# A recommender tower on one core: the first table part ahead of the ids, the first ids and the first one-hot in halves

## What is computed

```python
e = jnp.stack([tbl_0[ids[:, 0]], ..., tbl_39[ids[:, 39]]], axis=1)
xi = e[:, iidx, :]
xj = e[:, jidx, :]
z = jnp.einsum('bpd,pde,bpe->bp', xi, bilinear_matrices, xj)
h = jnp.concatenate([z, dense_ctx], axis=1)
h = jnp.maximum(h @ W_top1 + b_top1, 0.0)
h = jnp.maximum(h @ W_top2 + b_top2, 0.0)
y = h @ W_top3
```

## Time and profile before

| | |
|---|---|
| median of 3 runs | 189.72 us (189.65 to 190.01) |
| the profiled execution's own time | 189.45 us |
| its span, first to last instruction | 187.6 us |
| mean granted TensorE clock | 0.991 |
| busy PE, DVE, POOL, ACT | 93%, 79%, 56%, 28% of the span |

### The profile page before, as it was taken

One profiled execution on the slowest core, in us unless ns is written; L12 is line 12 of the kernel. 1 busy time (PEld: TensorE's weight loads), 2 busy tenths in 40 slices (PEclk: granted clock), 3 DMA queues, 4 the chain that ended last, 5 costly groups with the idle time before them and its releaser, 6 DMA issues.

```text
span 187.6 us, 4092 instructions
## 1 busy us (share of the span) xinstructions
PE 174.1 (93%) x1766; PEld 59.9 (32%) x1766; DVE 148.9 (79%) x147; ACT 52.9 (28%) x52; POOL 105.8 (56%) x114
## 2 busy tenths in 40 slices
PE   6789788889999999999999999799999997998992
PEld 6434323233332233232323323223323242332340
DVE  1898999989599899899899999768899985770502
ACT  3875596898100201112110111102110111111501
POOL 2687777877877777777777777778600022202000
PEclk9969999999999999999999999999999999999999
DMA  5996130341055970220000010000000000000000
GB/s 153 350 410 254 17 98 14 108 124 19 14 153 102 330 285 14 73 106 18 13 15 14 14 17 11 14 18 12 3 0 0 3 0 0 5 0 0 3 0 0
DMA packets 7786, 13.07 MB, mean 70 GB/s; under 512 B 2164, under 2 KB 4728, under 8 KB 7768
## 3 DMA queue, kind: packets, MB, share of 16 engines
q1 hardware_dynamic: 4552, 11.15, 17.2%
q0 software_dynamic: 3072, 1.58, 4.8%
q10 hardware_dynamic: 144, 0.08, 0.3%
HBM read 12.67 MB, written 0.00 MB: 68 GB/s over the span
## 4 chain that ended last, share of the span: by engine, by line
PE 84%; ACT 8%; DVE 3%; DMA 2%; issue 2%; DVEq 0%; ACTq 0%
PE ps_t L679 27%; PE ps_z L693 27%; PE ps_x L727 9%; PE ps_x L642 7%; PE ps_t L738 4%; PE ps_t L673 3%; ACT hot_act L508 3%; ACT hot_act L510 3%; DMA ids<-ids_oh 2%; PE ps_t L713 2%; PE ps_x L654 2%; PE ps_z L642 1%; PE ps_t L706 1%; DVE hot_dve L556 1%; PE ps_t L642 1%
## 5 line engine op out<-in xcount | busy, mean ns | idle before, releaser
L596 DVE TENSOR_TENSOR prod<-ps_t,xt 128x1024 f32<-128x1024 f32 x100 | 116.7, 1218 | 18.3 <-PE ps_t L679 15.6
L485 POOL DMA_INDIRECT emb<-tbl,idx x96 | 94.5, 985 | 32.8 <-issue 29.0
L679 PE MATMUL ps_t<-xt,w_sb 32*128 32x512 f32 x360 | 54.3, 640 | 0.0
L693 PE MATMUL ps_z<-prod,ones 128*32 128x512 f32 x400 | 53.3, 605 | 0.0
L493 POOL TENSOR_TENSOR late_z<-late_z,tbl_oh 128x512 f32<-128x512 f32 x8 | 10.2, 1289 | 30.6 <-ACT tbl_oh L537 30.6
L727 PE MATMUL ps_x<-late_z,late_w 128*32 128x256 f32 x320 | 22.6, 379 | 2.0 <-ACT tbl_oh L537 2.0
L679 PEld LDWEIGHTS ps_t<-xt,w_sb 32*128 32x128 f32 x360 | 16.6, 183 | 22.5 <-issue 15.0
L556 DVE TENSOR_SCALAR hot_dve<-ids,ramp 128x2048 bf16<-128x2048 int16 x26 | 18.6, 763 | 3.7 <-DMA ids<-ids_oh 3.7
L693 PEld LDWEIGHTS ps_z<-prod,ones 128*32 128x32 f32 x400 | 7.9, 108 | 38.2 <-DVE prod L596 22.1
L727 PEld LDWEIGHTS ps_x<-late_z,late_w 128*32 128x32 f32 x320 | 10.3, 110 | 20.9 <-issue 19.0
L508 ACT ACTIVATE hot_act<-ids,neg_ramp 128x2048 bf16<-128x2048 int16 x8 | 15.9, 1992 | 2.7 <-DMA ids<-ids_oh 2.7
(11 more groups left out here) (64 smaller groups left out, 92.1 us busy)
## 6 DMA issues: line engine op xcount, KB each, us to landing
ids<-ids_oh SPq DMA_DIRECT2D x4, 512.0 KB, 7.0
emb<-tbl,idx POOLq DMA_INDIRECT x96, 2.3
late_w<-w SPq DMA_DIRECT2D x1, 1280.0 KB, 8.4
tbl_oh<-small_tables SPq DMA_DIRECT2D x2, 512.0 KB, 8.0
w_sb<-w_pairs SPq DMA_DIRECT2D x1, 704.0 KB
tbl_oh<-small_tables SPq DMA_DIRECT2D x1, 640.0 KB, 11.3
w_sb<-w_pairs SPq DMA_DIRECT2D x1, 640.0 KB
w_sb<-w_pairs SPq DMA_DIRECT2D x1, 576.0 KB, 4.5
```

The costliest lines, as they stand in the source:

```text
L485: nc.gpsimd.indirect_dma_start(emb[:, n % E_RING, t, u * D:(u + 1) * D], None, tables[field], bass.IndirectOffsetOnAxis(ap=idx[:, at:at + ...
L596: nc.vector.tensor_tensor(prod[:, g % PROD_RING, :].rearrange("p (i b) -> p i b", i=2), ps_t[PAIR[g]][:, :].rearrange("p (i b) -> p i b", ...
L679: last = nc.tensor.matmul(o, w_sb[s * D:(s + 1) * D, at:at + P], xt[s * D:(s + 1) * D, kk, :], start=True, stop=True)
L693: last = nc.tensor.matmul(ps_z[q * D:(q + 1) * D, :], ones[:, v * D:(v + 1) * D], prod[:, t // 2 % PROD_RING, t % 2 * B:(t % 2 + 1) * B], ...
```

## The change

Block 0's ids come as two transfers, of two fields each (256 KB): the first on ACT's queue ahead of `idx`, the second on SP's. SP issues table part 0 first and the second half of the ids behind it; the rest of its order stays. DVE does the split of part 0 ahead of its first one-hot, and that one-hot as two instructions of 128 x 1024, each after its own half. TensorE waits for both (the first half has a semaphore of its own); ACT's first one-hot waits for both halves of the ids.

```diff
--- before.py
+++ after.py
@@ -376,6 +376,9 @@
         ones_zero, ones_made = sem("ones_zero"), sem("ones_made")
         ramp_made = sem("ramp_made")
         neg_ramp_made = sem("neg_ramp_made")
+        HALF_IDS = FB // 2 * B
+        first_ids_in = [sem(f"first_ids_in{half}") for half in range(2)]
+        first_hot_half = sem("first_hot_half")
         ids_oh_in = [sem(f"ids_oh_in{j}") for j in range(len(OH_BLOCKS))]
         tbl_in = [sem(f"tbl_in{n}") for n in range(len(TBL_PARTS))]
         tbl_rest_made, tbl_last_made = sem("tbl_rest_made"), sem("tbl_last_made")
@@ -415,6 +418,12 @@
         def hot_rows(j):
             return slice(OH_FIRST[j], OH_FIRST[j + 1])
 
+        def load_first_ids(engine, half):
+
+            cols = slice(half * HALF_IDS, (half + 1) * HALF_IDS)
+            engine.dma_start(ids_oh[:, 0, :, :].rearrange("p f b -> p (f b)")[:, cols],
+                             ids_oh_rows[0:1, cols].broadcast_to([P, HALF_IDS])).then_inc(first_ids_in[half], 16)
+
         @block.sync
         def _(sp):
             def load_weights(k):
@@ -428,8 +437,8 @@
                 sp.dma_start(ids_oh[:, j, :, :].rearrange("p f b -> p (f b)"),
                              ids_oh_rows[j:j + 1, :].broadcast_to([P, FB * B])).then_inc(ids_oh_in[j], 16)
 
-            load_small_ids(0)
             load_small_tables(0)
+            load_first_ids(sp, 1)
             load_small_tables(1)
             load_small_ids(1)
             load_small_tables(2)
@@ -500,7 +509,10 @@
             def one_hot(n):
 
                 j, c = ACT_HOTS[n]
-                if n == 0 or ACT_HOTS[n - 1][0] != j:
+                if n == 0:
+                    act.wait_ge(first_ids_in[0], 16)
+                    act.wait_ge(first_ids_in[1], 16)
+                elif ACT_HOTS[n - 1][0] != j:
                     act.wait_ge(ids_oh_in[j], 16)
                 wait_slot(act, ACT_HOTS, n, ACT_RING, hot_used_act)
                 o = hot_act[:, n % ACT_RING, :, :]
@@ -509,6 +521,7 @@
                 act.wait_ge(distance_made, n + 1)
                 nc.scalar.activation(o, o, ACT.Relu, bias=1.0, scale=-1.0).then_inc(hot_made_act, 1)
 
+            load_first_ids(act, 0)
             act.dma_start(idx[:, :], ids).then_inc(ids_in, 16)
             act.wait_ge(ramp_made, len(OH_BLOCKS))
             nc.scalar.activation(neg_ramp[:, :], ramp[:, :], ACT.Copy, scale=-1.0).then_inc(neg_ramp_made, 1)
@@ -549,7 +562,7 @@
             def one_hot(n):
 
                 j, c = DVE_HOTS[n]
-                if n == 0 or DVE_HOTS[n - 1][0] != j:
+                if DVE_HOTS[n - 1][0] != j:
                     dve.wait_ge(ids_oh_in[j], 16)
                 wait_slot(dve, DVE_HOTS, n, DVE_RING, hot_used_dve)
                 at = OH_FIRST[j] + c
@@ -572,8 +585,14 @@
                 nc.vector.memset(ones[g * D:(g + 1) * D, g::D + FB], 1.0).then_inc(ones_made, 1)
 
             dve.wait_ge(ramp_made, len(OH_BLOCKS))
-            one_hot(0)
             split_part(0)
+
+            assert DVE_HOTS[:3] == [(0, 0), (0, 1), (0, 2)]
+            for half, signal in enumerate((first_hot_half, hot_made_dve)):
+                fields = slice(half * FB // 2, (half + 1) * FB // 2)
+                dve.wait_ge(first_ids_in[half], 16)
+                nc.vector.tensor_scalar(hot_dve[:, 0, fields, :], ids_oh[:, 0, fields, :],
+                                        ramp[:, 0:1], None, ALU.is_equal).then_inc(signal, 1)
             one_hot(1)
             split_part(1)
             one_hot(2)
@@ -634,6 +653,8 @@
                         blocks, units = SHARED_BANK_WAITS.get(("hot", k), (0, 0))
                         if blocks:
                             pe.wait_ge(moved, blocks)
+                    if k == (0, 0):
+                        pe.wait_ge(first_hot_half, 1)
                     pe.wait_ge(made, n + 1)
                     cols = slice((OH_FIRST[j] + c) * FB * D, (OH_FIRST[j] + c + 1) * FB * D)
                     parts = [upper_halves(tbl_oh[0:OH_P, cols]), upper_halves(tbl_rest[0:OH_P, cols]), tbl_last[0:OH_P, cols]]
```

## The result

The changed kernel takes 190.1 us, the kernel before 189.67 (medians of 22 runs each, run in turn): ratio 1.0031, 95% interval 1.0017 to 1.0045. It is slower by 0.43 us where 0.69 less was forecast. Its runs fall in two groups: eleven of the 22 lie about 189.8, nine about 190.85, and two between. The profiled execution is of the upper group: 190.97 us, span 189.2. It is also the only one of the 22 with a mean granted clock under 0.996 (0.981), so it is not a typical run.

The account below looks back on a forecast made before the run. Block 0's end was taken to set the kernel's end, through DVE's start-up before TensorE's third chunk. Split hidden and one-hot halved, against ids 0.4 later, gained 0.69: 189.72 - 0.69 = 189.0 us, range 188.5 to 189.6.

Parts of the forecast that it names:

- When the ids land: Start-up loads: the last half of the ids lands at 5.67 us, 0.4 later than before, bounds 4.8 and 6.7.
- What the moved issues cost: ACT's queue and POOL's gathers: idx lands at 5.84 us instead of 5.44, all gathers 0.4 later, nothing lost.
- The slack of 1.39 us: Block 8: last gather there at about 110.65, transpose at 112.04; gain 0.69 and delay 0.4 use 1.09 of the slack.
- The sum on DVE: DVE's start-up steps behind the ids: TensorE's third chunk starts at 9.56 us instead of 10.25, gain 0.69 us.
- the clock stays up: Rival, start-up: TensorE keeps 2.4 GHz, ACT's second one-hot arrives last, gain 1.05 of which 1.0 passes: 188.7 us; chance 0.12.
- The slower rival: Rival, gathers: idx behind 256 KB on ACT's queue exceeds block 8's slack; idx at 7.25 gives 190.1 us; chance 0.08.

Follow-up runs that it names:

- e4: The kernel before with only the first table part ahead of the ids on SP and the first split ahead of the first one-hot; 189.33 us, ratio 0.9966.
- e7: The kernel before with the first table part moved from SP to ACT's queue behind idx, and the first split ahead of the first one-hot; 190.98 us, ratio 1.0064.
- e10: The kernel before with idx as SP's first transfer, ahead of the ids, instead of ACT's; 189.98 us, ratio 1.0014.
- r2: The kernel before once more, unchanged, for a second trace; 189.74 us.
- e13: The changed kernel with ACT issuing idx first and the first half of the ids behind it, in the same rounds as r3; median 189.95 us, ratio 1.0008.
- r3: The changed kernel itself, unchanged, run in the same rounds as e13; median 190.80 us, ratio 1.0050.
- e1: The changed kernel with ACT issuing idx first and the first half of the ids behind it; median 189.89 us, ratio 1.0006.
- e8: The changed kernel with SP issuing the second ids half before the table part, and DVE doing the half one-hots before the split; 190.67 us, ratio 1.0051.
- e5: The changed kernel with both halves of the ids on SP behind the first table part, ACT issuing idx alone; 191.16 us, ratio 1.0073.

## Why the prediction was wrong

*When the ids land.* This step failed: 0.4 us for 128 KB was taken from the 286 to 369 GB/s of the stretch 4 to 6 us. The last half came not 0.4 but 1.7 to 1.95 us later than before (7.0, 6.94 and 7.22 in three traces), outside the bounds. It is not only that there was more to move: less was moved. Between 2 and 6 us it was 0.95 to 1.01 MB in the three traces of the changed kernel, against 1.14 and 1.15 in the two of before. e4, e7 and e10 show the pattern: the ids land at 6.58 and 7.23 with 128 and 80 KB ahead of them on SP's queue (0.82 and 0.69 MB moved from 2 to 6 us), at about 6.0 with 128 KB beside them on ACT's, and at 5.3 without. Why that little costs that much stays open.

*What the moved issues cost.* The second failure. Idx was put at 5.84 with 6.74 as the upper bound; it landed at 7.1 to 7.41, 1.7 to 2.0 us later than before, behind 256 KB that themselves were slow.

*The slack of 1.39 us.* The third failure. The delay of idx alone is more than this slack, and the slack itself was not to be relied on: in the second trace of before TensorE already waits 1.15 us for the gathers. It was read from one execution in which the clock had fallen, block 0 was late and POOL was 1.37 us quicker to the 64th gather. It was read at block 8, too, where block 7 had less (1.2). One hint that this trace stood apart was there: it was 0.27 below the median.

*The sum on DVE.* The split left the path and the half one-hot was right (0.45 forecast, 0.48 measured). The second table part, put at 6.74, landed at 1.64 + 6.4 = 8.0; DVE reached its split only at 8.1, so that cost nothing. But with the clock up, ACT's four activations behind the ids end block 0, and they wait for the last half; taking 0.79 off DVE could gain nothing there. The rival "the clock stays up" named ACT's second one-hot as last to arrive; what it gave chance 0.12 is the usual case (21 of 22 runs with a mean clock of 0.996 or more).

*The slower rival* named the right mechanism (idx behind 256 KB, block 7 and 8) and was given 0.08, because idx was thought to land within 0.2 us of the ids. It did: but the ids themselves were late. That the rival's number, 190.1, is the measured median is luck: the median lies between two groups, and the slack it was worked out from was not there in r2. The swap of e13 against r3 shows that the place of idx costs the time, 0.4 to 0.85 us. That no gain stands against it is the ids' lateness: with idx early, e1 and e13 are level with before.

By the Trainium skill, page "DMA: Bandwidth & Descriptors", section "Rules for kernel authors", loads spread over several queues share the same engines and gain no bandwidth. e8 agrees: its halves land at 5.1 and 4.8 on two queues, the whole at 5.27 on one. e5 against the changed kernel does not bear this out (the last half at 8.22 on one queue, at 7.0 on two), but there idx changed its place as well.

In the two traces of before TensorE is given the same work at nearly the same times, and between 11 and 12 us the granted clock is 0.50 in one and 1.00 in the other. That fits the clock monitor of the Trainium skill, page "TensorE: Matmul & The Clock Gate", section "What's actually happening", which runs freely and does not restart with the kernel; the monitor itself no run here shows.

## What to carry over

A slack read from one trace belongs to that execution: where the profiled time lies off the median, take a second trace before costing anything against a slack. Transfers that several later chains start from (here 80 KB of indices for 96 gathers) must not stand behind bulk on their queue. Nor is the first place free: e4 gained with idx alone on ACT's queue, e10 did not with idx ahead of the ids on SP's. Before taking work off one engine's start, ask which other engine waits for the same load and what it has to do behind it.

## What was not expected

POOL's pace differs by over 1 us between executions of one program: the 64th gather issued 82.5 us after the first in one trace of before (5.71 to 88.24) and 83.9 in the other (5.72 to 89.61), with idx at the same place. The whole difference arises in the first 32 gathers (42.5 and 43.9 us); the next 32 take 40.0 us in both. Those first 32 run beside DVE's one-hots, and single ones take up to 1.77 us there, against 0.94 to 0.95 later. What sets the pace among them was not tried. And a wait of TensorE for a gather can cost twice: in e8's trace the clock reads 0.50 behind 1.8 us of waiting. That run took 192.12, and the five of its twelve runs with a mean clock of 0.988 to 0.991 took 191.99 to 192.14, where the seven with 0.996 or more took 189.49 to 190.72.
